# LSTM steps: the gates' input rows put in by four row groups at a step's end, 48 products ahead; attention's q inside the loop

## The reference, cut to what matters

```python
# LSTM; S = 4 cells, H = 512, one step per row of x
logits = concat([h, c, x_t]) @ W_sel.T + b_sel
s = argmax(logits)                      # one of four cells
g = x_t @ W_ih[s].T + h @ W_hh[s].T + b_ih[s] + b_hh[s]
i, f, g, o = split(g, 4)
c = sigmoid(f) * c + sigmoid(i) * tanh(g);  h = sigmoid(o) * tanh(c)

# attention; 8 heads of 64; weights of one of three sets, by a router
q, k, v = x @ wq, x @ wk, x @ wv
out = (softmax(q k^T / 8) v) @ wo
```

## Time and profile before

| | us |
|---|---|
| median of 3 runs | 5581.73 (5580.29 to 5581.82) |
| profiled execution | 5580.44, its span 5578.7 |
| TensorE, VectorE, ScalarE busy | 87%, 50%, 26% of the span |
| mean granted TensorE clock | 0.967 |

### The profile page before, as it was taken

One profiled execution on the slowest core, in us unless ns is written; L12 is line 12 of the kernel. 1 busy time (PEld: TensorE's weight loads), 2 busy tenths in 40 slices (PEclk: granted clock), 3 DMA queues, 4 the chain that ended last, 5 costly groups with the idle time before them and its releaser, 6 DMA issues. The chain is left out here.

```text
span 5578.7 us, 281252 instructions
## 1 busy us (share of the span) xinstructions
PE 4864.6 (87%) x116024; PEld 3179.5 (57%) x117274; DVE 2796.3 (50%) x11344; ACT 1427.0 (26%) x4662; POOL 633.1 (11%) x1073
## 2 busy tenths in 40 slices
PE   8999686999898997888888888888888888867789
PEld 6644343444565445666666666666666666645546
DVE  5500345232554664555555555555555555546614
ACT  0000000012232352333333333333333333323413
POOL 0000283000563110000000000000000000001200
PEclk9999897999999998999999999999999999989989
DMA  0000111167543851000000000000000000001000
GB/s 11 15 30 15 28 42 35 45 210 257 145 119 94 293 156 31 11 11 11 12 11 11 11 11 12 11 11 11 11 11 12 11 11 11 11 27 42 15 34 10
DMA packets 153467, 259.51 MB, mean 47 GB/s; under 512 B 47554, under 2 KB 81480, under 8 KB 149037
## 3 DMA queue, kind: packets, MB, share of 16 engines
q1 hardware_dynamic: 98344, 176.13, 9.5%
q0 software_dynamic: 55040, 82.30, 5.2%
HBM read 172.87 MB, written 85.14 MB: 46 GB/s over the span
## 5 line engine op out<-in xcount | busy, mean ns | idle before, releaser
L1583 PE MATMUL bank<-lstm_w,step_h_parts 128*32 128x128 f16 x94848 | 1557.6, 220 | 104.1 <-issue 7.0
L1583 PEld LDWEIGHTS bank<-lstm_w,step_h_parts 128*32 128x32 f16 x94848 | 1340.6, 97 | 455.4 <-issue 302.9
L1655 DVE TRANSPOSE_TENSOR_REDUCE step_summed<-bank 128x4 f32 (+1 forms) x2500 | 792.5, 317 | 1064.3 <-PE bank L1583 897.6
L1578 PE MATMUL bank<-step_xg,step_rows 128*128 (+1 forms) x1252 | 475.7, 381 | 277.3 <-issue 257.8
L1551 ACT ACTIVATE step_act_out<-step_summed,lstm_inv_scale 128x4 f32<-128x4 f32 x625 | 185.8, 297 | 1709.1 <-DVE step_summed L1655 1709.1
L1539 POOL COPY xnT<-step_state 128x4 f32 (+1 forms) x625 | 116.4, 186 | 2746.8 <-DVE step_state L1680 2746.8
L1204 PE MATMUL bank<-sum_parts,sum_hot 125*125 125x512 f16 x1600 | 347.9, 381 | 6.9 <-DVE sum_parts L1160 6.9
L1204 PEld LDWEIGHTS bank<-sum_parts,sum_hot 125*125 125x125 f16 x1600 | 219.4, 137 | 135.8 <-DVE sum_parts L1160 7.7
L1454 PE MATMUL bank<-xg_w,xnT 128*125 128x512 f32 x640 | 277.0, 596 | 6.6 <-DMA xg_w<-in_c_w_ih 6.6
L553 POOL DMA_INDIRECT gcn_rows<-gcn_h_rows,gcn_idx x160 | 201.6, 1260 | 696.8 <-issue 696.5
L1578 PEld LDWEIGHTS bank<-step_xg,step_rows 128*128 128x128 bf16 x2500 | 142.3, 97 | 210.2 <-issue 131.0
(11 more groups left out here) (365 smaller groups left out, 6238.8 us busy)
## 6 DMA issues: line engine op xcount, KB each, us to landing
rel_h<-rel_h_sb SPq DMA_DIRECT2D x39, 1024.0 KB, 6.4
lstm_xg<-cnt POOLq DMA_DIRECT2D x80, 375.0 KB, 4.1
step_xg<-lstm_xg SPq DMA_DIRECT2D x375, 80.0 KB
xg_w<-in_c_w_ih SPq DMA_DIRECT2D x16, 1024.0 KB
lstm_w<-in_c_w_hh SPq DMA_DIRECT2D x16, 1024.0 KB, 12.7
cheb_w<-in_L_gnn_weight SPq DMA_DIRECT2D x8, 1024.0 KB
choose_we<-in_L_ffn_experts SPq DMA_DIRECT2D x8, 1024.0 KB
rel_bases<-in_L_gnn_bases SPq DMA_DIRECT2D x8, 1024.0 KB, 10.6
```

The lines of the kernel that those rows point to most:

```text
L1578: return nc.tensor.matmul(bank[:], rows[:, p, :], xg[:, at, :], start=True, stop=stop)
L1583: last = nc.tensor.matmul(bank[32 * q:32 * q + 32, 128 * s:128 * s + 128], h_parts[:, c, :], w[:, s, c, q, a, 128 * p:128 * p + 128], star ...
L1655: nc.vector.tensor_reduce(summed[:, 4 * p:4 * p + 4], bank[:, bass.ds(s * 128, 128)].rearrange("p (b r) -> p b r", r=32), X_AXIS, ALU.add, ...
```

## The change

Ring and constant. The ring's partitions are laid out anew: gate p has partitions 32 p to 32 p + 23, twelve rows of the three input parts of its four cells and twelve of bias. `rows` becomes one 128x128 matrix. SyncE loads a chunk with 12 DMAs of four partitions instead of 3 of 16, and the bias with 4 instead of 1. It refills a slot by `row_ready` instead of `injected`.

Row. ScalarE copies the next step's 128x512 slice of the ring into a fixed tile `row`, at the end of `activate`, when the injects that read the row before are done.

Inject. Each inject is a matmul of 24 partitions in row group p, with `tile_position=(32 p, 0)`. All four stand at the end of the step, in the order f, g, i, o, each behind its `summed_*`; none is left ahead of the choice.

Ahead. The products ahead take three halves instead of two, 48 products; the cell has 20 for f.

Counts. VectorE's decrements move from ahead of the f reduce to behind the reduces.

Attention. q is computed a row tile at a time into bank 7: the first tile ahead of the loop, the others inside it; v comes behind the first scores, in banks 4, 5 and 6.

```diff
-XG_ROWS = GATES * 4 * 3
+XG_ROWS = 4 * 3
+AHEAD_HALVES = 3
...
             def load(k, slot):
-                for a in range(3):
-                    sp.dma_start(xg[16 * a:16 * a + 16, bass.ds(slot * XG_CHUNK, XG_CHUNK), :],
-                                 B.xg[:, bass.ds(k * XG_CHUNK, XG_CHUNK), a, :]).then_inc(xg_loaded, 16)
+                for p in range(GATES):
+                    for a in range(3):
+                        at = 32 * p + 4 * a
+                        sp.dma_start(xg[at:at + 4, bass.ds(slot * XG_CHUNK, XG_CHUNK), :],
+                                     B.xg[4 * p:4 * p + 4, bass.ds(k * XG_CHUNK, XG_CHUNK), a, :]).then_inc(xg_loaded, 16)
...
-                sp.wait_ge(injected, (k - (XG_SLOTS - 1)) * XG_CHUNK - 1)
+                sp.wait_ge(row_ready, (k - (XG_SLOTS - 1)) * XG_CHUNK)
...
                 nc.scalar.activation(tc[:], state[:, 0:4], ACT.Tanh).then_inc(tc_ready, 1)
+                if ahead and not last:
+                    act.wait_ge(xg_loaded, ((n + 1) // XG_CHUNK + 1) * XG_DONE)
+                    act.wait_ge(injected, n)
+                    nc.scalar.copy(row[:], xg[:, next_row(n), :].rearrange("p t k -> p (t k)")).then_inc(row_ready, 1)
...
-            def inject(part, at, stop):
+            def inject(part, stop):
                 p, bank, _, _ = part
-                return nc.tensor.matmul(bank[:], rows[:, p, :], xg[:, at, :], start=True, stop=stop)
+                held = slice(32 * p, 32 * p + 2 * XG_ROWS)
+                return nc.tensor.matmul(bank[:], rows[held, :], row[held, :], start=True, stop=stop,
+                                        tile_position=(32 * p, 0))
...
-                    for c, a in halves[2 if part is part_f else 0:]:
+                    for c, a in halves[AHEAD_HALVES if part is part_f else 0:]:
...
-            def inject_f_g(t):
-                at = bass.ds(t % XG_RING, 1)
-                for part in (part_f, part_g):
+            def inject_all(t):
+                pe.wait_ge(row_ready, t + 1)
+                for part in parts:
                     pe.wait_ge(part[3], t)
-                    inject(part, at, stop=False)
-
-            def inject_i_o(t):
-                at = bass.ds(t % XG_RING, 1)
-                for part in (part_i, part_o):
-                    pe.wait_ge(part[3], t)
-                    last = inject(part, at, stop=False)
+                    last = inject(part, stop=False)
                 last.then_inc(injected, 1)
...
                 for s in range(CELLS):
-                    for a in range(2):
-                        add_half(part_f, s, 0, a, stop=False)
-                inject_i_o(t)
+                    for c, a in halves[0:AHEAD_HALVES]:
+                        add_half(part_f, s, c, a, stop=False)
...
                 if ahead:
-                    inject_f_g(t + 1)
+                    inject_all(t + 1)
...
-                s = dve.value_load(pick[0:1, 0:1], min_val=0, max_val=CELLS - 1)
-                dve.sem_inc(score_done, -1)
-                dve.sem_inc(top_ready, -1)
-                parts_taken()
-                return s
+                return dve.value_load(pick[0:1, 0:1], min_val=0, max_val=CELLS - 1)
...
                 add_rows(part_f, s, n)
+                dve.sem_inc(done_f, -1)
                 if t is not None:
                     dve.sem_inc(picked, -1)
                 add_rows(part_g, s, n)
+                dve.sem_inc(done_g, -1)
+                if t is not None:
+                    dve.sem_inc(score_done, -1)
                 forget(n)
                 add_rows(part_i, s, n)
+                dve.sem_inc(done_i, -1)
+                if t is not None:
+                    dve.sem_inc(top_ready, -1)
                 add_rows(part_o, s, n)
+                dve.sem_inc(done_o, -1)
                 new_i(n)
...
+            def queries(m):
+                if m >= 3:
+                    pe.wait_ge(added, m - 2)
+                for n in range(KC):
+                    for c in range(KC):
+                        last = nc.tensor.matmul(B.bank[7][:, n * R:(n + 1) * R], wq[:, c, n * 128:(n + 1) * 128],
+                                                xnT[:, c, m * R:(m + 1) * R], start=(c == 0), stop=(c == KC - 1))
+                last.then_inc(q_done, 1)
...
+            pe.wait_ge(wq_loaded, 16)
+            queries(0)
+            pe.wait_ge(k_kept, KC)
+            pe.wait_ge(k_tail_kept, KC)
             scores(0)
             scores(1)
-            pe.wait_ge(v_kept, NT + 1)
-            pe.wait_ge(wo_loaded, 16)
+            pe.wait_ge(wv_loaded, 16)
+            for m in range(NT):
+                values(m)
+            pe.wait_ge(v_kept, NT)
             for i in range(M + 1):
...
                 if i >= 1:
                     sum_values(i - 1)
+                if i < M and i % AH == 0 and i // AH + 1 < NT:
+                    queries(i // AH + 1)
```

More of the change, by code:

```diff
@@ L1494, in lstm_steps @@
         xg = sb("xg", [128, XG_RING, 512], BF16)
-        rows_f = sb("rows_f", [128, GATES, 128], F32)
-        rows = sb("rows", [128, GATES, 128], BF16)
+        row = sb("row", [128, 512], BF16)
+        rows_f = sb("rows_f", [128, 128], F32)
+        rows = sb("rows", [128, 128], BF16)
         state = sb("state", [128, 8], F32)
@@ L1521, in _ @@
             sp.wait_ge(cleared, 1)
-            sp.dma_start(xg[64:64 + XG_ROWS, :, :], bias_rows.to_broadcast((XG_ROWS, XG_RING, 512))
-                         ).then_inc(bias_loaded, 16)
+            for p in range(GATES):
+                at = 32 * p + XG_ROWS
+                sp.dma_start(xg[at:at + XG_ROWS, :, :],
+                             bias_rows[p * XG_ROWS:(p + 1) * XG_ROWS].to_broadcast((XG_ROWS, XG_RING, 512))
+                             ).then_inc(bias_loaded, 16)
             for slot in range(XG_SLOTS):
@@ L1546, in _, with activate @@
         def _(act):
-            def activate(n, ahead=True, last=False):
-                if ahead and not last:
-                    act.wait_ge(xg_loaded, ((n + 1) // XG_CHUNK + 1) * XG_DONE)
+            def activate(n, first=False, ahead=True, last=False):
                 act.wait_ge(summed_f, n)
@@ L1561, in activate @@
                 act.wait_ge(summed_o, n)
+                if first:
+                    nc.scalar.copy(row[:], xg[:, 1, :]).then_inc(row_ready, 1)
                 nc.scalar.activation(act_out[:, 12:16], summed[:, 12:16], ACT.Sigmoid, scale=L.inv[:, 0:1]
@@ L1565, in activate, with next_row @@
                 nc.scalar.activation(tc[:], state[:, 0:4], ACT.Tanh).then_inc(tc_ready, 1)
+                if ahead and not last:
+                    act.wait_ge(xg_loaded, ((n + 1) // XG_CHUNK + 1) * XG_DONE)
+                    act.wait_ge(injected, n)
+                    nc.scalar.copy(row[:], xg[:, next_row(n), :].rearrange("p t k -> p (t k)")).then_inc(row_ready, 1)
+            def next_row(n):
+                return bass.ds((n + 1) % XG_RING, 1)
+            act.wait_ge(bias_loaded, 16 * GATES)
+            act.wait_ge(xg_loaded, XG_DONE)
+            nc.scalar.copy(row[:], xg[:, 0, :]).then_inc(row_ready, 1)
             act.wait_ge(lx_loaded, 16)
-            activate(1)
+            activate(1, first=True)
             with act.Fori(1, STEPS - 2) as t:
@@ L2152, in routed_attention @@
     P_SLOTS = 3
+    V_BANK = (4, 5, 6, 4, 6)
     def score_big(i):
@@ L2289, in _, with keep_q @@
             nc.scalar.activation(score[:], logit[:], ACT.Exp, bias=neg_top[:]).then_inc(exp_done, 1)
-            for n in range(2 * KC):
-                act.wait_ge(qk_done, n + 1)
-                dst = (kT, qT)[n // KC]
-                nc.scalar.copy(dst[:, n % KC, 0:500], B.bank[2 * (n % 2)][:, 0:500]).then_inc(qk_kept, 1)
+            for n in range(KC):
+                act.wait_ge(k_done, n + 1)
+                nc.scalar.copy(kT[:, n, 0:500], B.bank[2 * (n % 2)][:, 0:500]).then_inc(k_kept, 1)
+            def keep_q(m):
+                act.wait_ge(q_done, m + 1)
+                nc.scalar.copy(qT[:, :, m * R:(m + 1) * R], B.bank[7][:, 0:500].rearrange("p (c r) -> p c r", c=KC)
+                               ).then_inc(q_kept, 1)
             def expo(i):
@@ L2321, in _ @@
                     expo(i + 2)
+                if i % AH == 0 and i // AH + 1 < NT:
+                    keep_q(i // AH + 1)
                 if i >= AH and i % AH == 2:
```

82 lines of the change are left out of this document (41 added, 41 removed).

## The result

| | before | after |
|---|---|---|
| median | 5581.01 us (5580.19 to 5581.82, 4 runs) | 5805.74 us (5802.85 to 5806.61, 4 runs) |
| ratio after to before | | 1.040 (95%: 1.0387 to 1.0412) |
| span of the profiled execution | 5578.7 us | 5804.8 us |
| mean granted TensorE clock | 0.967 | 0.943 |
| step at the full clock, mean | 4.516 us | 4.682 us |

The kernel is 225 us slower. The forecast was 132 us slower, and the time lies outside the range that was given. Nearly all of it is in the LSTM: from the first step to the last 3052.1 us against 2834.8 (+217.3), its start about +6.2. The stages ahead of it, which the change doesn't touch, differ by 4.7; what follows it by -2.0, of which attention is -0.7.

The account below looks back on a forecast made before the run. It took the LSTM step's ring to be set by answers TensorE waits for and by its sequencer. +0.20 us a step x 623 = +125, with +6 and +1 gives +132: 5713 us, own range 5680 to 5755, 5530 to 5755 with rival A.

Parts of the forecast that it names:

- The hold: At the loop's end, TensorE's sequencer waits at o's inject for the o reduce, so scores start 0.29 us later.
- Rival A: At the loop's end, the sequencer goes past a waiting inject, so the kernel gets faster: 5548 us; chance 0.17.
- Products ahead: Ahead of the choice, 48 products make the cell one round shorter, -0.056 us; the index read 0 to 0.05 us late.
- Idle array ahead of the cell: Before the cell's first load, injects in row groups no longer hold the array: -0.03 us a step (0 to -0.06).
- the step at the full clock: One LSTM step, sum of its terms: +0.29 - 0.056 - 0.03 = +0.20 us (0.15 to 0.27).
- The clock: TensorE's granted clock in the LSTM loop, taken to stay at 1.00, with no cost in the sum.
- Rival B: Less array work a step makes the clock fall to 1.2 GHz inside the loop: +930 us, 6640 us; chance 0.03.
- Start of the LSTM: SyncE's added row and bias loads and the first row copy delay the first products: +6 us once (3 to 8).
- Attention: q moved from the prologue into the loop, v filling TensorE's waits: +1 us in sum (-3 to +4).
- ScalarE's row copy: Copy of 128x512 behind the tanh, about 0.6 us, covered by 2 us before the next sigmoid: 0.
- VectorE's counts: Decrements moved behind the reduces: the f reduce 0.07 us earlier plus its round, but later gates wait for TensorE: 0.

Follow-up runs that it names:

- e3: Kernel before with one wait changed: the step's last inject, gate g's, waits for the o reduce instead of the g reduce; 5731.1 us.
- e7: Kernel before with 48 products ahead instead of 32 and the cell's f shorter by four; 5684.9 us.
- e1: Changed kernel with o's inject alone moved out of the loop's end, behind the 48 products ahead; 5584.6 us.
- e12: Changed kernel's row groups, row copy, counts and attention, but injects placed as in the kernel before and 32 products ahead; 5656.8 us, 1.013 of before.
- e11: Against e6, only the injects' form differs: through the whole array one after another instead of in row groups; 5564.6 us, 0.9969 of before.
- e2: Changed kernel, same inject place and order, but each inject a 128-partition matmul through the whole array, one after another; 5704.4 us.
- e6: Changed kernel with o's inject behind the products ahead, and three halves ahead for cells 0 and 2, two for 1 and 3 (40 products); 5572.2 us.
- e4: Changed kernel plus two filler products of zeros, 512 columns each, behind the products ahead; 5711.2 us.
- e9: Against e5, one filler product of zeros with 512 columns added behind o's inject; 5629.5 us, 1.0084 of before.
- e10: Against e6, one filler product of zeros with 256 columns added behind o's inject; 5609.1 us, 1.0049 of before.
- e8: Changed kernel plus eight filler products of zeros, four columns each, behind the products ahead; 5797.5 us.
- e5: Changed kernel with o's inject behind the products ahead, and 32 products ahead instead of 48; 5657.2 us, 1.0123 of before.

## Why the prediction was wrong

**The hold: right in mechanism and size.** Forecast +0.29 us on the score (0.26 to 0.32), measured +0.278 in after and +0.273 in e3. The loop's arithmetic, branch and move stand behind the waiting inject on the sequencer, as the earlier trace rows had shown in one step. Rival A falls: its sign was a loop addition ahead of the o reduce's end, and it came 0.05 us behind it in every step at the full clock, in after and in e3. The wait queue of the Trainium skill (Perfetto Trace Analysis, Per-engine timelines), by which the sequencer is free for the next instruction while one waits, isn't what TensorE shows here.

**Products ahead: right in this order, wrong as a general statement.** From the cell's first product to the o reduce the step became 0.055 us shorter (1.914 to 1.859), as forecast (0.056). That 48 products let the sequencer go at most 0.05 us late doesn't hold where the index is early: e7 shows 0.22, e1 0.07. The forecast rested on "nothing if it is", that is if the choice is later than today, and that was so. What is not shown is why e7 loses more than e1; e7 has one more inject ahead of the read, and each goes through the whole array.

**Idle array ahead of the cell: the right sign, too small.** Forecast -0.03 us; the way from the index's read to the cell fell by 0.049. Where the gain comes from is not separated: e3, which keeps both injects ahead of the cell and only has the later index, has 0.032 of it, and e12, which keeps the early index and has the row groups, 0.042.

**So the step at the full clock** was forecast at +0.20 (0.15 to 0.27) and is +0.166: 0.270 - 0.049 - 0.055. By these terms alone the time would have been about 5690 us, inside the forecast's own range.

**The clock: the step that failed.** In the sum of the forecast the clock stands at nothing. Rival B was named and given 3 in 100, with the words "the idle stretches stay under 1 us, and the loop now holds 1.00 throughout". Both hold, and neither speaks for the changed kernel. That before held 1.00 says how things stand with its work, not how much of it can be taken away. The change takes three of four 512-column injects out of the array's time, 0.66 us a step by my own sum, and lengthens the step; I priced only what this gives and not what it puts at risk. B was also priced as all or nothing (6640 us). It came in a quarter of the steps: 301 us of half clock in 85 stretches, 110 us of the time, and that is what carries the time from 5690 to about 5800 and out of the range.

That the form of the injects is what costs the clock is shown within one batch: e12, with the row groups, fell (0.942 to 0.947), while before, which has their order without them, and e11, which has everything else of the change but the hold and eight of the 48 products, held theirs beside it (0.966 to 0.968 and 0.965 to 0.967). The pairs that differ in the form alone agree, but each spans two batches: after and e2 (301 and 21 us of half clock), e6 and e11 (109 and 16). That it is by the array work which the form takes away is the reading that fits the filler: with two products of 512 columns (e4: 17), one of 512 (e9: 24) or one of 256 (e10: 26) the half clock goes, with eight of 4 columns it stays (e8: 275). The idle stretch ahead of the cell isn't the cause by itself: in e12 it is 0.45 us in the mean and in before, where the clock holds, 0.47; and long ones without the row groups went with 21 and 24 us of half clock (e2 and e3, 0.70 and 0.69 us).

The Trainium skill (TensorE: Matmul & The Clock Gate, Part 1: The HAM clock gate) describes a clock that follows how busy TensorE has lately been. These runs agree, and add that it isn't read off the profile's busy column: after shows 170 us of 200 busy at 0.93 and e6 183 at 0.97, where e2 and e11 show 168 at 1.00. In part that is because the column gives each of the injects side by side 0.41 us, about as much as a single one (0.38), and because e2's trace lacks a quarter of its injects' matmul records.

What stays open: what the four stretches of products and idle in a step must look like for the clock to hold. Between e1, e6 and e5 the half clock grows as the array work shrinks: 164 products a step (48 and 116), about 158 and 152 (32 and 120), and 26, 109 and 267 us. after has e1's 164 products in a step that is 0.175 us longer, and 301 us. That fits missing array work and is no proof: the spread of the work within the step changes with it, and e1 ran on another chip than e5 and e6. None of the four kernels of e1's batch lost its clock, so the chip isn't ruled out, and e1 to e4 show less by their high clock than the others do. The kernel before isn't far from the edge either: one of its 13 executions beside e5 to e8 took 5615.3 us at a granted clock of 0.959, the others had 0.965 to 0.968. And why one step falls and its like doesn't (3059.05 and 3063.78 above) the trace doesn't tell.

**The small terms.** Start of the LSTM about +6.2 us (forecast +6). Attention -0.7 us (forecast +1, -3 to +4). ScalarE's row copy takes 0.617 us a step and delays nothing: the next sigmoid waits for the f reduce as before, and tanh and h_weight end where they did (0.833 and 0.856 us behind the start of the o reduce). VectorE's counts: f's reduce comes 0.083 us sooner after the cell, 0.056 of it for the round and 0.027 for the counts (e12, with before's 24 products, has 0.575 us where before has 0.602), not the 0.07 forecast; the later gates gain nothing by it. None of these was run alone; they are read from the traces.

```profile
L1576 ACT COPY step_row<-step_xg 128x512 bf16 (+1 forms) x623 | 384.6, 617 | 107.3 <-PE bank L1596 49.5
```

## What to carry to other kernels

Where a loop that waits more than it computes holds TensorE's full clock, its array work can be part of what holds it: before work is packed, shortened or moved out of the array, ask what the clock will do, and price a clock that falls in some of the steps, not only in all. A wait at the end of TensorE's loop was paid with everything queued behind it, the loop's own branch included; put the instruction that waits longest behind the work that needn't wait. And products that fill idle array time were only free while the sequencer was done handing them over before it had to read the next decision.

## What the runs showed of the hardware that was not expected

- Four products of 24 partitions side by side let the clock fall (301 us of half clock), where four of 128 partitions with the same result, one after another, held it (21 us), at the same place in a step of nearly the same length (4.682 and 4.699 us): a form that takes less of the array's time and made the kernel 101 us slower.
- Eight products of 4 columns fill 0.35 us of the profile's busy time and do nothing for the clock (275 us of half clock against 301); two of 512 columns do (17 us).
- TensorE's sequencer reads a register 0.07 to 0.22 us late when 48 products instead of 32 stand ahead of the read (e1, e7), and on time with 40 and one inject (e6).
